# Second layer norm in an attention and expert kernel: scale and shift formed for two tiles at once, one round later

## What is computed

```python
h = _layernorm(x, axis=-1) * (1 + ca) + sa
x = x + ga * attention(h, ...)
h = _layernorm(x, axis=-1) * (1 + cb) + sb      # the second norm
x = x + gb * experts(h, ...)
# _layernorm: m = mean(x); v = var(x); (x - m) / sqrt(v + 1e-05)
```

## Time and profile before

| | us |
|---|---|
| median of three runs | 1293.57 |
| the profiled execution | 1293.22 |
| its span, first to last instruction | 1291.4 |
| outside the span | 1.8 |
| DVE busy in the span | 906.8 |
| POOL busy in the span | 929.5 |
| PE busy in the span | 1152.0 |
| last instruction of the attention stage on DVE (L162) | 668.56 |

### The profile page before, as it was taken

How to read it: one execution, slowest core, us unless ns; L and a number is a source line. 1 busy time by engine, 2 the same in 40 slices (tenths; PEclk the granted TensorE clock), 3 DMA queues, 4 the chain that set the end, 5 groups by cost and what they waited for, 6 DMA issues and landing times. The chain is left out here.

```text
span 1291.4 us, 53384 instructions
## 1 busy us (share of the span) xinstructions
PE 1152.0 (89%) x19576; PEld 978.8 (76%) x19576; DVE 906.8 (70%) x2387; ACT 713.2 (55%) x1419; POOL 929.5 (72%) x990
## 2 busy tenths in 40 slices
PE   4699999999999999999623899999999999999995
PEld 1477778888777777787413788888888888888884
DVE  2589999999999999999888544444444444444442
ACT  2378888988889888898533233333333333333331
POOL 3168999999899999999822466666666667676653
PEclk8599999999899999999655999999999999999998
DMA  8323343334333334333355688878788887888860
GB/s 223 82 69 82 94 138 116 90 106 123 100 104 111 106 108 118 97 118 101 100 155 148 124 137 128 136 136 134 137 135 137 127 131 136 133 139 136 136 108 1
DMA packets 201704, 153.07 MB, mean 119 GB/s; under 512 B 101658, under 2 KB 179570, under 8 KB 201330
## 3 DMA queue, kind: packets, MB, share of 16 engines
q0 software_dynamic: 32592, 56.75, 27.4%
q1 hardware_dynamic: 160770, 81.89, 25.0%
q10 hardware_dynamic: 8096, 11.01, 3.3%
HBM read 63.58 MB, written 44.04 MB: 83 GB/s over the span
## 5 line engine op out<-in xcount | busy, mean ns | idle before, releaser
L1298 PE MATMUL psum<-xT,xall 128*128 128x256 f16 x3408 | 384.8, 273 | 14.9 <-DMA xT<-grow 14.9
L1298 PEld LDWEIGHTS psum<-xT,xall 128*128 x3408 | 334.0, 98 | 54.3 <-issue 15.2
L1360 POOL DMA_INDIRECT out<-late,sidx x142 | 227.0, 1599 | 167.0 <-DVE late L1349 80.1
L1306 ACT ACTIVATE sg<-psum 128x512 f32<-128x512 f32 x142 | 84.8, 597 | 281.6 <-PE psum L1298 281.6
L1311 DVE SCALAR_TENSOR_TENSOR late<-psum,sg 128x512 f32<-128x512 f32 x142 | 98.2, 692 | 185.0 <-ACT sg L1306 182.9
L1278 POOL DMA_INDIRECT grow<-moe_rows,gidx x142 | 146.1, 1029 | 86.9 <-DVE gidx L1150 44.0
L1332 PE MATMUL psum<-w2s,hT 128*128 x1704 | 197.7, 273 | 2.8 <-DVE w2s L1386 2.6
L1332 PEld LDWEIGHTS psum<-w2s,hT 128*128 128x128 f16 x1704 | 166.6, 98 | 22.8 <-issue 3.4
L1322 DVE TENSOR_TENSOR hT<-late,hT 128x512 f16<-128x512 f32 x142 | 98.4, 693 | 98.7 <-ACT hT L1318 98.7
L1318 ACT ACTIVATE hT<-late 128x512 f16<-128x512 f32 x142 | 89.4, 629 | 112.0 <-DVE late L1311 112.0
L672 POOL TENSOR_TENSOR pT<-sc,pT 128x1024 f16<-128x1024 f32 x64 | 136.5, 2134 | 11.7 <-ACT pT L668 11.7
(11 more groups left out here) (262 smaller groups left out, 2294.2 us busy)
## 6 DMA issues: line engine op xcount, KB each, us to landing
stk<-qk SPq DMA_DIRECT2D x384, 64.0 KB, 2.9
moe_rows<-hrows SPq DMA_DIRECT2D x64, 256.0 KB, 3.6
out<-xall SPq DMA_DIRECT2D x64, 128.0 KB, 3.3
raw<-in_w ACTq DMA_DIRECT2D x26, 256.0 KB, 3.3
xall<-in_x ACTq DMA_DIRECT2D x16, 256.0 KB, 4.0
raw<-in_w SPq DMA_DIRECT2D x8, 512.0 KB, 8.9
xall<-in_x SPq DMA_DIRECT2D x8, 384.0 KB, 8.1
grow<-moe_rows,gidx POOLq DMA_INDIRECT x142, 4.7
```

The lines of the kernel that those rows point to most:

```text
L1298: i = k.e.matmul(bank[:, n * LONG:(n + 1) * LONG], w13s[:, bass.ds(ex_reg * (G * 4 * I) + ((2 * c + b_) * 2 * I + col), P)], xT[:, k.x, a, ...
L1306: done(k.e.activation(sg[:, half, :], bGate[half][:, :], ACT.Silu, scale=1.0 / W_SCALE), "sg")
L1360: k.e.indirect_dma_start(out_rows, bass.IndirectOffsetOnAxis(ap=sidx[:, n:n + 1], axis=0), yo[:, k.v, q, :], None, bounds_check=B * T - 1, ...
```

## The change

`var_eps2`, `ln2_scale` and `ln2_shift` return at once for an even tile; for an odd tile they work on two columns, its own and that of the tile before. `ln2_shift` becomes a scalar_tensor_tensor, since two tiles can't share one scale per partition: its inputs are `mv2` and `rstd2`, both in SBUF. The semaphores of the three stages count pairs. Everything behind them runs one round later, and the tables of which reader frees a PSUM bank are moved with it. The attention stage has one round more at its end.

```diff
     PER_SEGMENT = ("eps", "pow", "nmr")
+    PER_TWO = ("ep2", "pw2", "nm2")
...
-            return S[stage], (of // NJ if stage in PER_SEGMENT else of) + 1
+            return S[stage], of // (NJ if stage in PER_SEGMENT else 2 if stage in PER_TWO else 1) + 1
...
+    def two(k):
+        return slice(k.j - 1, k.j + 1)
     def var_eps2(k):
+        if k.t % 2 == 0:
+            return
         k.wait("ag2")
         k.wait("xn2", 4)
-        done(k.e.tensor_scalar(rstd2[:, k.j, :], mv2[:, k.j, 1:2], EPS_LN, None, ALU.add), "ep2")
+        done(k.e.tensor_scalar(rstd2[:, two(k), 0], mv2[:, two(k), 1], EPS_LN, None, ALU.add), "ep2")
     def ln2_scale(k):
+        if k.t % 2 == 0:
+            return
         k.wait("ep2")
-        done(k.e.tensor_tensor(rstd2[:, k.j, :], rstd2[:, k.j, :], mhalf[:, 0:1], ALU.pow), "pw2")
+        done(k.e.tensor_tensor(rstd2[:, two(k), 0], rstd2[:, two(k), 0], mhalf[:, 0:2], ALU.pow), "pw2")
     def ln2_shift(k):
+        if k.t % 2 == 0:
+            return
         k.wait("pw2")
         k.wait("xn2", 4)
-        done(k.e.tensor_scalar(nmr2[:, k.j, :], mv2[:, k.j, 0:1], rstd2[:, k.j, :], -1.0, ALU.mult, ALU.mult), "nm2")
+        done(k.e.scalar_tensor_tensor(out=nmr2[:, two(k), 0], in0=mv2[:, two(k), 0], scalar=-1.0, in1=rstd2[:, two(k), 0],
+                                      op0=ALU.mult, op1=ALU.mult), "nm2")
...
-                  (8, softmax_exp), (8, p_high), (5, h1t), (12, ln2_act), (17, logit_copy), (6, sk_act),
-                  (7, max_high), (13, rows_hi), (3, ln_act), (15, h2_act), (6, v_high)],
+                  (8, softmax_exp), (8, p_high), (5, h1t), (13, ln2_act), (18, logit_copy), (6, sk_act),
+                  (7, max_high), (14, rows_hi), (3, ln_act), (16, h2_act), (6, v_high)],
```

More of the change, by code:

```diff
@@ L416, in attention @@
         "h2Tr": ((("lg", 2),),
-             (("h2T", 1), ("gat", -4),)),
+             (("h2T", 1), ("gat", -5),)),
         "mTr": ((("mx", 0),),
@@ L429, in attention @@
              (("exp", 1),)),
-        "Wo": ((("h2T", 5),),
-             (("gat", 1), ("lg", 7),)),
+        "Wo": ((("h2T", 6),),
+             (("gat", 1), ("lg", 8),)),
         "T1": ((("aT", 6),),
@@ L437, in attention @@
              (("umul", 1),)),
-        "rtr": ((("gat", -6),),
+        "rtr": ((("gat", -7),),
              (("h2T", -1), ("lg", 1),)),
@@ L875, in attention @@
     program = {
-        "sync": [(4, stack_low), (3, stack_high), (13, store)],
-        "tensor": [(2, mem_mm), (11, h2_trans), (3, max_trans), (2, proj_v), (1, proj_qk), (4, pv), (6, a_trans),
-                  (3, scores_by_key), (6, w_o), (0, t1), (2, scores), (3, update), (12, router)],
+        "sync": [(4, stack_low), (3, stack_high), (14, store)],
+        "tensor": [(2, mem_mm), (12, h2_trans), (3, max_trans), (2, proj_v), (1, proj_qk), (4, pv), (6, a_trans),
+                  (3, scores_by_key), (6, w_o), (0, t1), (2, scores), (3, update), (13, router)],
         "vector": [(2, aggr), (9, mem_av), (0, stats), (9, v_rest), (9, v_new), (11, pv_den),
@@ L883, in attention @@
         "scalar": [(6, qk_high), (6, qk_relu), (10, a_high), (11, a_act), (0, var_eps), (6, qk_exp),
-                  (8, softmax_exp), (8, p_high), (5, h1t), (12, ln2_act), (17, logit_copy), (6, sk_act),
-                  (7, max_high), (13, rows_hi), (3, ln_act), (15, h2_act), (6, v_high)],
-        "gpsimd": [(12, p_rest), (8, ln_mult), (16, ln2_mult), (17, rows_lo), (15, ln2_scale), (12, update_add),
-                  (13, a_rest), (16, ln2_add), (3, ln_scale), (12, a_add), (14, res_add), (3, ln_shift)],
+                  (8, softmax_exp), (8, p_high), (5, h1t), (13, ln2_act), (18, logit_copy), (6, sk_act),
+                  (7, max_high), (14, rows_hi), (3, ln_act), (16, h2_act), (6, v_high)],
+        "gpsimd": [(12, p_rest), (8, ln_mult), (17, ln2_mult), (18, rows_lo), (15, ln2_scale), (12, update_add),
+                  (13, a_rest), (17, ln2_add), (3, ln_scale), (12, a_add), (14, res_add), (3, ln_shift)],
     }
```

## The result

The changed kernel takes 1299.31 us (median of 18 runs, 1294.26 to 1304.16) against 1291.64 us of the kernel before beside it (18 runs): a ratio of 1.0064, 95% interval 1.0050 to 1.0078, so 6.5 to 10 us slower. The forecast was 1304.7 us with its own range of 1298 to 1309. The profiled execution took 1300.82 us (span 1299.0), 7.6 us more than that of before.

A forecast was written before the change was run, and what follows sets the result against it. DVE was taken to bound the attention stage, POOL's position being set anew each round by the gate product. Terms 3.2 + 9.9 - 1.6 = +11.5 us gave 1304.7 us, own range 1298 to 1309, 8 in 10 range 1289 to 1309.

The forecast's parts named there:

- What bounds the stage: Attention stage: DVE fills the round, 132.96 of 138 us and 175.86 of 182; POOL waits 0.46 us for the gate product.
- That both wide instructions wait: Two-column add and two-input shift on DVE wait for POOL's instruction in progress; the add up to 0.47 us.
- Rivals 2 and 3: Attention stage: 2, only the shift waits, 1291.6 us, chance 0.16; 3, nothing waits, about 1283 us, chance 0.12.
- rival 4: Waits fall where DVE would have waited for PE anyway, nothing is left: 1293 us, chance 0.06.
- rival 2's sum: Only the shift waits: pair without weights -0.28 us; in all -2.2 + 2.2 - 1.6 = -1.6 us; chance 0.16.
- Rounds without weights: 95 to 336 us: full round +0.74, empty -0.34, together +0.40 a pair; 8 pairs from 198 give +3.2 us.
- Rounds with a weight part: 357 to 594 us: add and shift wait, L78 loses its turn; four rounds +1.53, 26 rounds +9.9 us.
- the step that failed: Full weight rounds: behind the add POOL's L840 goes first, so L78 ends one L840 later, +0.68 us.
- rival 1: Waits are there, but L78 goes through right behind the add: +3.8 us, 1297 us, chance 0.22.
- The step that the shift waits for the end of L518: Every second full weight round: L518 (1.02 us) follows L843 without a pause and holds the shift, +0.72 us.
- The first weight part: First L78, 2.41 us before: its alignment with POOL is gone, -1.6 us, bounds -2.4 and 0.
- The end: The round more lengthens the last logits' chain by 2.2 us, hidden by 6.6 us before DVE's placing ends.

The follow-up runs named there:

- narrow shift: Changed kernel with the pair's shift formed by two one-column instructions, one tensor and one number per partition, the add still two columns wide: 1291.06 us, ratio 0.9997 to before.
- the one without pairs: Against the kernel before: ACT adds eps and negates the mean, POOL raises and multiplies, tile by tile, everything behind one round later: 1284.07 us, ratio 0.9934.

## Why the prediction was right, and where its size was off

**What bounds the stage** was read rightly in the main: POOL's wait in front of L814, nearly all of it for the gate product, grew from 34.0 us over the run to 43.4, and the kernels that free DVE are the fast ones. What it left out is how near PE is (below).

**That both wide instructions wait** was right, for the reason given. The shift takes 0.66 to 0.73 us in 15 of the 18 full rounds from 200 to 540 and ends with L853 (forecast: the end of L843). The add takes 0.42 to 0.51 in most weight rounds (0.47 at most was forecast from rows) but only some 0.2 in most rounds without, where DVE arrives later in L532. Rivals 2 and 3 fall by this, and rival 4, no change in time, by the ratio. (In rival 2's sum the pair comes to -0.26, not -0.28 us, which changes nothing.)

**Rounds without weights:** +3.2 forecast, +6.4 measured, 2.9 of it in the two rounds with the late transfer. The other seven pairs have +0.5 each where +0.40 was forecast, but shared out in another way. Three `row_max` in a row on the timeline,

```profile
251.56 1.21 DVE L628 TENSOR_REDUCE mx<-psum 128x16 f32<-128x1024 f32 x1
...
260.22 1.23 DVE L628 TENSOR_REDUCE mx<-psum 128x16 f32<-128x1024 f32 x1 [0.33 <-PE psum L621]
...
269.09 1.22 DVE L628 TENSOR_REDUCE mx<-psum 128x16 f32<-128x1024 f32 x1
```

are 8.66 and 8.87 us apart where 8.52 was usual; 9.3 and 8.2 had been forecast. PE does not let the empty round be shorter: DVE waits for it at the end of one, 0.33 us in the middle row, and nine times in the stretch, 4.4 us. So the empty rounds give nothing back, and the full ones are lengthened by less than DVE waits in them. How the wait is shared between the two I infer, no run isolates it. The prediction had the number for it: it says that PE leaves 0.17 us of a round to be had, and then takes 0.34 off the empty one. Most of these rounds last 8.43 or 8.44 us in the kernel with nothing of this on DVE, where PE is the bound, so 8.2 was not to be had. With 0.17 in its place the pair would have come to 0.74 - 0.17 = +0.57, an estimate; +0.50 was measured.

**Rounds with a weight part** hold the step that failed: "L840 is at hand and goes next (L121 and L122 again); L78 ends one L840 later". It doesn't; L78 took 0.49 to 0.51 us right behind the add in all 13 full rounds from 371 to 594, as rival 1 had it. By the prediction's own words it was wrong if L78's mean did not rise: that mean fell from 0.90 to 0.73 us. The run that holds L78 back shows how little was missing, 0.10 us. The nearest rows were not near enough: L122 started 0.02 us behind POOL's instruction, L78 here 0.00 to 0.03 ahead of it. The step that the shift waits for the end of L518, +0.72, failed too; it was inferred from POOL's long tensors, and four columns don't hold the shift. Over the same 26 rounds the stage lost 240.5 - 236.6 = +3.9 us, against the forecast's +9.9 and rival 1's +2.2. Full and empty rounds alternate at about 9.6 and 8.9 to 9.0 us; over 9.7 and under 9 was forecast.

**The first weight part** gave 2.7 us with the round behind it; 1.6 was forecast, and 2.4 was its bound. In the kernel with the narrow shift L78 took 2.60 us there again, so this is luck of alignment and no merit of the change. **The end** stayed hidden, with 5.2 us between the last logits and L162.

**The sum** with the measured terms, 1.2 + 6.4 - 2.7 + 3.9 - 0.6 (the last rounds) = +8.2, lies between rival 1 (+3.8) and the forecast (+11.5). The median, 1299.31, is 2.3 us above rival 1's 1297 and 5.4 below the forecast. The direction stood on the right mechanism, the wait of the wide shift; that of the add is there too, but beside a narrow shift no loss from it can be measured (0.9997). That the time also fell into the stated range is in part luck: the weight rounds were put 6.0 us too high, by the hand-over between two neighbouring DVE instructions and by the wait for L518, and the rounds without weights brought 3.2 more than forecast, 2.9 of it around 215, for which the forecast had no term. It stays open why the rounds near 215 were late: PE waited once there for `stk`, 1.6 us in the profile of the changed kernel and 1.4 in that of the one that holds L78 back, against 0.2 in the whole stretch before. Such waits come in the fast kernels too (4.2 us over the stage in the one without pairs), so they can't be put down to the wide instructions.

## What to carry to other kernels

Count what an instruction fetches before you merge it with its neighbour: on DVE, a one-column operation with one tensor input passes beside a busy POOL, while two columns or a second SBUF input wait for most of POOL's instructions. The shift's wait cost more here than the instruction saved; the paired add alone, beside a narrow shift, cost nothing measurable and saved nothing either. If such an instruction is needed, put it where POOL waits for DVE or is in an instruction that does not hold it off, or move it to an engine with idle time. Fewer instructions are worth something only on the engine that bounds the round.

## What the runs showed of the hardware

- Of two back-to-back DVE instructions that both wait for POOL, the second kept the turn (L78 in 0.50 us behind the add), and POOL's next was stretched instead (0.72 to 1.07 us); with 0.10 us between them it lost the turn (0.93 us).
- A waiting DVE instruction can lose several turns: 2.23 us behind three POOL instructions, until POOL itself had to wait. It had asked 0.16 us ahead of POOL's next start, in the end of `p_rest`; an add of the changed kernel that asked 0.15 ahead (263.29), in the end of L532, got through in 0.21. What decides this stays open.
- POOL's pow on four columns (1.01 us) did not hold off a two-input instruction, neither 0.06 us behind its start (0.16 us, where L78 is held back) nor in its middle (0.15 us, 12 times, with the shift two instructions later).
- The pow costs 568 ns for one column, 727 for two and 1024 for four.
